# Perceiver block: cross-attention with smaller TensorE tiles for the scores and the weighted sums

## The chip, the core and the metric

The kernel runs on one core of a Trainium2 chip. The metric is the device time of one execution in microseconds (us), as the median over several runs.

## What is computed

A block of three layers works on `x` of 16 batch elements x 64 queries x 512. Only the first layer is touched, a cross-attention of 16 heads of 32 dimensions to a context of 1601 rows of 256 per batch element:

```python
y_dca, y_main = y[:, -16:], y[:, :-16]                 # 16 and 1585 context rows
k, v = (y_main @ Wk + bk), (y_main @ Wv + bv)           # per head, k is layer-normed over its 32 dimensions
ctx = softmax(q @ k.T * 32 ** -0.5) @ v                 # q is layer-normed per head too
ctx = ctx + softmax(q @ k_dca.T * 32 ** -0.5) @ v_dca   # the 16 last rows, with weights of their own
return ctx @ Wo + bo
```

A self-attention with 4 key heads and a mixture of 8 experts (2 for each token) follow.

## The kernel before

All of it is float32. The projections of the context are made from three products of halves in a reduced form (`split_product`, line 107); scores, transposes and weighted sums are plain float32 matmuls, each of which the trace shows as two pairs of one weight load (PEld, LDWEIGHTS) and one MATMUL.

`cross_attention` works through the 16 batch elements, two in a step i. The context of one element is cut into chunks of 128 keys: 12 full ones and a *tail* with what is left of the main rows and the 16 `dca` rows. Such a chunk is a *unit* u; a step has 26 units, of which 24 are full chunks and two are tails. Both tails share one projection. The units are taken in 12 *groups* a step: five groups of two units and one of three (the third is the tail) for each element. The table `GROUP` at the top of the file holds them.

Each engine has its own order of work, written out by hand in its `steps`, and semaphores join them. In the PE stream one group is: key projection, value projection and transposes of the normalised keys (`keys`, `values`, `turn`) for later groups; then the weighted sums (`weighted`, L1296) of this group's units, then the scores (`scores`, L1279) of the next group's units. ACT makes the exponentials of a group (`exps`, L1004) first of all in its turn, then copies values (L990), scales and stores the transposed keys (L976), rounds the context (L963) and gives the seeds of the reciprocal roots (L113, L115). DVE adds the key bias (L1133), reduces the squares (L1139) and normalises (L120 to L124, L1148). POOL squares (L1088) and makes the low halves of the context (L1081).

For a unit the scores are transposed: the stationary operand is the keys, the moving one the queries. `k32` holds 128 rows (4 heads x 32 dimensions), 4 groups of heads, 128 keys. `qbd` holds the queries in a block-diagonal form: rows of head r have their 64 queries in the column half r % 2 and zeros in the other half. A matmul takes 64 rows (two heads), 128 keys and 128 columns of `qbd`, and gives the scores of two heads: 8 matmuls a unit, alternating between the row tiles of rows 0 to 63 and 64 to 127. They fill two PSUM banks for 16 heads x 64 queries. The first unit of a group uses banks 3 and 4, the second 5 and 6, the tail 1 and 2, which are the value and transpose banks. An exponential of 128 x 1024 turns a unit's two banks into `probs`.

For the weighted sums the probabilities are stationary (128 keys x 64 queries of one head) and the values with a column of ones move (33 columns). Heads 2p and 2p + 1 go to the two column tiles of 64. That is 16 matmuls for a chunk and 32 for a tail, where the main rows and the `dca` rows are summed apart. Chunks accumulate in bank 7.

The kernel has a second form of its loops, taken when scores could grow large (`guarded`); the inputs here take the plain form, in which the PE program is written out for all steps.

A wait that the prediction speaks of, in the PE stream of groups 5 and 11 (the group after the scores of three units), before the first value projection into bank 1:

```python
if j == 0 and group in (5, 11):
    pe.wait_ge(s["ex"], unit(i, GROUP[group][-1]))
values(i, project[j])
```

Of the kernel before, what the change touches and what calls it, by code (L numbers as in the profile page):

```python
# [14 lines left out]
ACT = mybir.ActivationFunctionType  # L15
# [6 lines left out]
P = 128  # L22
B, SQ, D = 16, 64, 512
SK, DC, DCA = 1601, 256, 16
H, HD = 16, 32
# [10 lines left out]
GROUPS = H // 4  # L36
VW1 = HD + 1
VBUFS = 6
TAIL_ROWS, DCA_ROWS = (0, 64), (DCA_ROW, 0)
TAIL, PROJ, UNITS = LAST, 2 * CH - 1, 2 * CH  # L40
# [14 lines left out]
SCALE = HD ** -0.5  # L55
# [29 lines left out]
def transposes(pe, bank, src, ident, n=KD):  # L85

    for k in range(n):
        last = pe.transpose(bank[:, k * P:(k + 1) * P], src[:, k * P:(k + 1) * P], ident)  # L88
    return last
# [655 lines left out]

def cross_attention(nc, io, g, psum):
    K_BANK, V_BANK, TR_BANK, S_BANK, O_BANK = 0, 1, 2, 3, 7
    S_PLACES = (S_BANK, S_BANK + 2, V_BANK)

    with ExitStack() as ctx:  # L750
        def sb(name, shape, dt=F32):
            return ctx.enter_context(nc.sbuf_tensor(name, shape, dt))

        s = Sems(nc, ctx, "xa")
# [8 lines left out]
        k32 = g.k32  # L763
        probs = sb("probs", [P, 3, H * SQ])
        select = sb("select", [2, 3, P])
        shift_raw = sb("shift_raw", [2, H * SQ])
        shift = sb("shift", [2, H * SQ])
# [5 lines left out]
        def at(i, n, per):  # L773

            return (i, n) if n < per else (i + 1, n - per)

        def projected(i, n):

            i, n = at(i, n, PROJ)
            return i * PROJ + (PROJ + n + 1)  # L780

        def unit(i, u):

            i, u = at(i, u, UNITS)
            return i * UNITS + (UNITS + u + 1)

        def column(n):

            return n if n < CH else n - CH

        def proj_of(u):

            return TAIL if u == UNITS - 1 else u

        def tail(n):

            return column(n) == LAST

        def buf(n):

            return 2 if tail(n) else column(n) % 2

        def k_buf(u):

            return {TAIL: 2, UNITS - 1: 3}.get(u, column(u) % 2)
# [5 lines left out]
        def last_unit(u):  # L811

            return u - UNITS + CH if u == TAIL else u - CH if u == UNITS - 1 else u - 2 if column(u) >= 2 else u - 3
# [30 lines left out]
        blocks = [(slice(i * HD, (i + 1) * HD), slice(i % 2 * SQ, (i % 2 + 1) * SQ)) for i in range(4)]  # L844

        def parts(guarded):

            return 5 if guarded else 4

        def place(h):  # L850

            return (h // 2 % 2) * 8 + h // 4 * 2 + h % 2

        def projections(group, room):

# [19 lines left out]
        with nc.Block() as block:  # L875
# [69 lines left out]
            def _(act):  # L945
# [52 lines left out]
                               projected(i, n)).then_inc(s["kseed"], 1)  # L998

                def exps(i, u, j):  # L1000
                    act.wait_ge(s["sc"], unit(i, u))
                    act.wait_ge(s["pv"], unit(i, last_unit(u)))
                    bank = S_PLACES[j]
                    nc.scalar.activation(probs[:, buf(u), :], psum[:, bank:bank + 2, :].rearrange("p a n -> p (a n)"),  # L1004
                                         ACT.Exp, scale=SCALE).then_inc(s["ex"], 1)

                def o_evac(b, i, u):

# [216 lines left out]
            def _(pe):  # L1225
# [20 lines left out]
                def turn(i, n):  # L1246
# [2 lines left out]
                    pe.wait_ge(s["ke"], projected(i, n - 1))  # L1249
                    transposes(pe, psum[:, TR_BANK, :], kn[:, buf(n), :], g.ident[:]).then_inc(s["tr"], 1)  # L1250

                def scores(i, u, j, guarded, values_done=None, turned_done=None):
                    i, u = at(i, u, UNITS)
                    b = i * 2 + u // CH
                    pe.wait_ge(s["ke"], projected(i, proj_of(u)))
                    if j < 2:
                        pe.wait_ge(s["ex"], unit(i, u - 3 if column(u) < 2 else u - 2))
                    else:
                        pe.wait_ge(s["ve"], values_done)
                        pe.wait_ge(s["ke"], turned_done)  # L1260
                    if column(u) == 0:
                        pe.wait_ge(s["qb"], b * parts(guarded) + parts(guarded))
                        if guarded:
                            pe.wait_ge(s["select"], 16)
                    if tail(u):
                        pe.wait_ge(s["kd"], b + 1)
                    bank = S_PLACES[j]
                    out = [[psum[:, bank + a, n * P:(n + 1) * P] for a in range(2)] for n in range(GROUPS)]
                    if guarded:

                        for n in range(GROUPS):
                            for a in range(2):
                                pe.matmul(out[n][a], select[:, {TAIL: 1, UNITS - 1: 2}.get(u, 0), :],
                                          shift[:, (2 * n + a) * P:(2 * n + a + 1) * P],
                                          start=(n == 0), stop=False, skip_group_check=True)
                    for n in range(GROUPS):
                        for a in range(2):
                            rows = slice(a * 2 * HD, (a + 1) * 2 * HD)
                            last = pe.matmul(out[n][a], k32[rows, k_buf(u), n, :], g.qbd[rows, n, :],  # L1279
                                             start=not guarded, stop=True, skip_group_check=True)  # L1280
                    last.then_inc(s["sc"], 1)

                def weighted(i, u, latest):
                    half = u // CH
                    pe.wait_ge(s["ex"], unit(i, u))
                    pe.wait_ge(s["ve"], projected(i, latest if tail(u) else u))
                    if column(u) == 0:
                        pe.wait_ge(s["oe"], i * 2 + (half + 1))
                    if tail(u):
                        pe.wait_ge(s[f"vd{half}"], i * 16 + 16)  # L1290
                    for n in range(2 if tail(u) else 1):
                        for p in range(PAIRS):
                            for j in range(2):
                                h = 2 * p + j
                                v = g.v_last[:, half, n, h, :] if tail(u) else g.v[:, (u - half) % VBUFS, h, :]
                                last = pe.matmul(psum[j * SQ:(j + 1) * SQ, V_BANK if n else O_BANK, p * VW1:(p + 1) * VW1],  # L1296
                                                 probs[:, buf(u), place(h) * SQ:(place(h) + 1) * SQ], v,
                                                 start=(p == 0 and (column(u) == 0 or n == 1)), stop=tail(u), skip_group_check=True)
                    last.then_inc(s["pv"], 1)

                def turn_ctx(b):
# [26 lines left out]
                def steps(i, room, guarded):  # L1328
                    latest = PROJ - 1
                    for group in range(GR):  # L1330
# [28 lines left out]
                        for u in units(group, room):  # L1359
                            weighted(i, u, latest)  # L1360
                        for j, u in enumerate(units(group + 1, room)):
                            scores(i, u, j, guarded, projected(i, latest), projected(i, last_turned))
# [1184 lines left out]
```

## Time and profile before

| | |
|---|---|
| median of 3 runs | 1488.43 us (1487.6 to 1489.63) |
| profiled execution, span from first to last instruction | 1487.2 us |
| PE busy, matmuls | 1399.9 us (94%), 15754 matmuls |
| PE busy, weight loads | 1181.9 us (79%) |
| DVE, ACT, POOL busy | 860.5, 778.8, 500.8 us (58, 52, 34%) |
| mean granted TensorE clock | 0.977 of 2.4 GHz |

The profile gives no separate time for the profiled execution; its span is 1.2 us under the median of the runs. Times are microseconds unless marked ns. PE is the matmul side of TensorE, PEld its weight loads, which overlap; DVE is VectorE, ACT ScalarE, POOL GpSimd. A form such as 128*64 128x33 says: 128 rows and 64 columns of the array, moving operand of 128 partitions x 33 elements. The duration of a single matmul holds its way through the array too, so starts tell more than durations. A row of the timeline merges like instructions that follow each other, from the first start to the last end.

### The profile page before, as it was taken

What the parts mean: (1) busy time and instruction counts of PE and PEld (TensorE: products, weight loads), DVE (VectorE), ACT (ScalarE), POOL (GpSimd) and SP (SyncE); (2) the same over time, 40 slices, a digit from 0 to 9 for tenths busy, and PEclk for the clock granted to TensorE, in tenths of its full rate; (3) what the DMA queues carried; (4) which work ended last, traced back from release to release, by engine and by line L of the source; (5) the groups of instructions that cost most, each with busy time, mean ns of one, the idle gap of its engine ahead of it and who ended that gap; (6) DMA issues with size and microseconds to landing.
All of it is one profiled execution on the core that took longest, in us unless ns stands there. A gap on an engine that the chain in (4) does not pass through costs nothing. (4 is left out here: it accounts for less than half of the span.)

```text
span 1487.2 us, 41615 instructions
## 1 busy us (share of the span) xinstructions
PE 1399.9 (94%) x15754; PEld 1181.9 (79%) x15754; DVE 860.5 (58%) x2005; ACT 778.8 (52%) x1560; POOL 500.8 (34%) x550
## 2 busy tenths in 40 slices
PE   6789999999999999999999999999999899984796
PEld 3378888888888888888888888888878677764696
DVE  7756555655655565556456555655555356655764
ACT  2345555655555565555555555555555433333653
POOL 3333333333333333333333333333323121111455
PEclk9999999999999999999999999999999999995999
DMA  7042110210111121102101101211010100004886
GB/s 253 19 158 77 31 30 16 91 31 16 62 46 30 30 78 30 30 16 92 30 16 62 48 28 30 78 30 31 17 74 2 60 3 30 30 30 178 220 182 140
DMA packets 38937, 91.24 MB, mean 61 GB/s; under 512 B 8135, under 2 KB 11722, under 8 KB 37258
## 3 DMA queue, kind: packets, MB, share of 16 engines
q1 hardware_dynamic: 31904, 72.38, 14.5%
q0 software_dynamic: 6432, 16.32, 4.8%
q8 instruction: 133, 2.18, 0.6%
q14 instruction: 34, 0.28, 0.1%
q10 hardware_dynamic: 434, 0.08, 0.0%
HBM read 71.93 MB, written 36.01 MB: 73 GB/s over the span
## 5 line engine op out<-in xcount | busy, mean ns | idle before, releaser
L1088 POOL TENSOR_TENSOR ksq<-kc 128x512 f32<-128x512 f32 x200 | 208.4, 1042 | 423.8 <-DVE kc L1133 421.9
L1133 DVE TENSOR_TENSOR kc<-psum,bk_sb 128x512 f32<-128x512 f32 x200 | 138.3, 692 | 235.2 <-PE psum L107 234.7
L990 ACT COPY v_sb<-psum 128x512 f32<-128x512 f32 x192 | 112.7, 587 | 277.2 <-PE psum L107 277.2
L1004 ACT ACTIVATE probs<-psum 128x1024 f32<-128x1024 f32 x208 | 201.0, 1023 | 76.6 <-PE psum L1279 76.5
L1081 POOL TENSOR_TENSOR y_lo<-y_sb,y_hi 128x256 fp32r<-128x256 f32 x190 | 139.8, 736 | 231.4 <-ACT y_hi L963 231.3
L1279 PE MATMUL psum<-qbd,k 64*128 64x128 f32 x3328 | 211.9, 278 | 0.1
L1296 PEld LDWEIGHTS psum<-v_sb,probs 128*64 128x64 f32 x6144 | 187.4, 138 | 18.5 <-issue 18.5
L1139 DVE TENSOR_REDUCE kss<-ksq 128x16 f32<-128x512 f32 x200 | 136.5, 682 | 111.4 <-POOL ksq L1088 111.4
L1296 PE MATMUL psum<-v_sb,probs 128*64 128x33 f32 x6144 | 198.1, 224 | 0.0
L1279 PEld LDWEIGHTS psum<-qbd,k 64*128 64x128 f32 x3328 | 193.3, 188 | 4.5 <-ACT k L976 0.3
L107 PE MATMUL psum<-wk_hi,y_hi 128*128 128x512 f32 x400 | 176.8, 442 | 10.7 <-issue 8.6
L107 PE MATMUL psum<-wv_hi,y_hi 128*128 128x512 f32 x400 | 158.1, 395 | 2.9 <-ACT v_sb L990 2.2
L107 PE MATMUL psum<-wk_hi,y_lo 128*128 128x512 f32 x400 | 158.0, 395 | 0.0
L107 PE MATMUL psum<-wk_lo,y_hi 128*128 128x512 f32 x400 | 157.1, 393 | 0.0
L107 PE MATMUL psum<-wv_hi,y_lo 128*128 128x512 f32 x400 | 156.9, 392 | 0.0
L107 PE MATMUL psum<-wv_lo,y_hi 128*128 128x512 f32 x400 | 156.4, 391 | 0.0
L976 ACT ACTIVATE k<-psum,cols_sb 128x512 f32<-128x512 f32 x192 | 150.6, 784 | 10.6 <-PE psum L88 10.6
L1148 DVE SCALAR_TENSOR_TENSOR kn<-kc,kr 128x512 f32<-128x512 f32 x200 | 141.5, 707 | 7.0
L88 PEld LDWEIGHTS psum<-ident_sb,kn 128*128 128x128 f32 x800 | 98.9, 139 | 26.6 <-issue 0.5
L88 PE MATMUL psum<-ident_sb,kn 128*128 128x128 f32 x800 | 119.8, 272 | 0.0
L122 DVE SCALAR_TENSOR_TENSOR ktmp<-ktmp,kseed 128x16 f32<-128x16 f32 x200 | 115.6, 578 | 6.8
L107 PEld LDWEIGHTS psum<-wk_hi,y_hi 128*128 128x128 f32 x400 | 75.5, 189 | 29.3 <-issue 11.1
(272 smaller groups left out, 1983.9 us busy)
## 6 DMA issues: line engine op xcount, KB each, us to landing
y_sb<-in_y SPq DMA_DIRECT2D x48, 512.0 KB, 3.6
slots_dram<-in_blank SPq DMA_DIRECT2D x9, 2080.0 KB
expert_raw<-in_experts SPq DMA_DIRECT2D x8, 1024.0 KB, 6.9
x_sb<-slots_dram SPq DMA_DIRECT2D x23, 260.0 KB, 3.2
x_sb<-in_x SPq DMA_DIRECT2D x1, 1536.0 KB, 10.7
wq<-in_wq SPq DMA_DIRECT2D x4, 256.0 KB, 4.4
xa_wo<-in_wo SPq DMA_DIRECT2D x1, 1024.0 KB, 12.1
y_tail<-in_y_tail SPq DMA_DIRECT2D x8, 128.0 KB, 21.2
```

The costliest lines, as they stand in the source:

```text
L88: last = pe.transpose(bank[:, k * P:(k + 1) * P], src[:, k * P:(k + 1) * P], ident)
L107: last = pe.matmul(bank, lhs, rhs, start=(n == 0), stop=(n == len(todo) - 1))
L122: nc.vector.scalar_tensor_tensor(out=tmp, in0=tmp, scalar=-0.5, in1=seed, op0=ALU.mult, op1=ALU.mult).then_inc(second, 1)
L976: last = nc.scalar.activation(k32[:, buf(n)], bank, ACT.Identity, scale=g.cols[:, 2:3], bias=g.cols[:, 3:4])
L1004: nc.scalar.activation(probs[:, buf(u), :], psum[:, bank:bank + 2, :].rearrange("p a n -> p (a n)"), ACT.Exp, scale=SCALE).then_inc(s["ex" ...
L1081: nc.gpsimd.tensor_tensor(g.y_lo[:, buf(n)], src, g.y_hi[:, buf(n)].bitcast(F32), ALU.subtract).then_inc(s["ylo"], 1)
L1088: nc.gpsimd.tensor_tensor(sq[:, buf(n)], kc[:, buf(n)], kc[:, buf(n)], ALU.mult).then_inc(s["ksq"], 1)
L1133: nc.vector.tensor_tensor(kc[:, buf(n)], psum[:, K_BANK, :], g.bk[:], ALU.add).then_inc(s["kb"], 1)
L1139: nc.vector.tensor_reduce(ss[:, buf(n)], head_view(sq[:, buf(n)]), AX_X, ALU.add).then_inc(s["krd"], 1)
L1148: nc.vector.scalar_tensor_tensor(out=head_view(kn[:, buf(n)]), in0=head_view(kc[:, buf(n)]), scalar=HD ** 0.5, in1=spread(kr[:, buf(n)], H ...
L1279: last = pe.matmul(out[n][a], k32[rows, k_buf(u), n, :], g.qbd[rows, n, :], start=not guarded, stop=True, skip_group_check=True)
L1296: last = pe.matmul(psum[j * SQ:(j + 1) * SQ, V_BANK if n else O_BANK, p * VW1:(p + 1) * VW1], probs[:, buf(u), place(h) * SQ:(place(h) + 1 ...
```

## The change

The weighted sums take 32 queries as stationary columns instead of 64, so that four column tiles are used in turn, with twice the matmuls, for chunks and tails. The scores of full chunks take 32 rows (one head) and 64 keys as stationary and only the 64 columns of `qbd` that are not zero as moving operand: 32 matmuls a unit instead of 8, over four row tiles and two column tiles. The scores of row tile r go to a bank of their own, 3 + r, and the two units of a group share these four banks, by column halves. The order of heads in `probs` changes with it. As the banks are shared, the exponential of a group's first unit waits for the scores of its second, and the scores of a group's first unit wait for the exponential of the last chunk before. Tails keep the old form of scores, in banks 1 and 2.

```diff
-    S_PLACES = (S_BANK, S_BANK + 2, V_BANK)
+    TAIL_BANK = V_BANK
...
-        def place(h):
-
-            return (h // 2 % 2) * 8 + h // 4 * 2 + h % 2
+        def place(h, u):
+
+            return (h // 2 % 2) * 8 + h // 4 * 2 + h % 2 if tail(u) else h % 4 * GROUPS + h // 4
...
                 def exps(i, u, j):
-                    act.wait_ge(s["sc"], unit(i, u))
+                    act.wait_ge(s["sc"], unit(i, u + 1 if j == 0 else u))
                     act.wait_ge(s["pv"], unit(i, last_unit(u)))
-                    bank = S_PLACES[j]
-                    nc.scalar.activation(probs[:, buf(u), :], psum[:, bank:bank + 2, :].rearrange("p a n -> p (a n)"),
-                                         ACT.Exp, scale=SCALE).then_inc(s["ex"], 1)
+                    if tail(u):
+                        out, scored = probs[:, buf(u), :], psum[:, TAIL_BANK:TAIL_BANK + 2, :].rearrange("p a n -> p (a n)")
+                    else:
+                        out = probs[:, buf(u), :].rearrange("p (r n) -> p r n", r=4)
+                        scored = psum[:, S_BANK:S_BANK + 4, j * GROUPS * SQ:(j + 1) * GROUPS * SQ]
+                    nc.scalar.activation(out, scored, ACT.Exp, scale=SCALE).then_inc(s["ex"], 1)
...
+                def chunk_scores(u, j, guarded):
...
+                    at_n = [slice(j * GROUPS * SQ + n * SQ, j * GROUPS * SQ + (n + 1) * SQ) for n in range(GROUPS)]
...
+                    for n in range(GROUPS):
+                        for half in range(2):
+                            keys = slice(half * SQ, (half + 1) * SQ)
+                            for r in range(4):
+                                rows, cols = blocks[r]
+                                last = pe.matmul(psum[keys, S_BANK + r, at_n[n]], k32[rows, k_buf(u), n, keys],
+                                                 g.qbd[rows, n, cols], start=not guarded, stop=True, skip_group_check=True)
+                    return last
...
-                    if j < 2:
-                        pe.wait_ge(s["ex"], unit(i, u - 3 if column(u) < 2 else u - 2))
-                    else:
+                    if j == 0:
+                        pe.wait_ge(s["ex"], unit(i, u - 2 if column(u) == 0 else u - 1))
+                    if j == 2:
                         pe.wait_ge(s["ve"], values_done)
                         pe.wait_ge(s["ke"], turned_done)
...
+                    last = tail_scores(u, guarded) if tail(u) else chunk_scores(u, j, guarded)
                     last.then_inc(s["sc"], 1)
...
-                                last = pe.matmul(psum[j * SQ:(j + 1) * SQ, V_BANK if n else O_BANK, p * VW1:(p + 1) * VW1],
-                                                 probs[:, buf(u), place(h) * SQ:(place(h) + 1) * SQ], v,
-                                                 start=(p == 0 and (column(u) == 0 or n == 1)), stop=tail(u), skip_group_check=True)
+                                for part in range(0, SQ, HD):
+                                    last = pe.matmul(psum[j * SQ + part:j * SQ + part + HD, V_BANK if n else O_BANK, p * VW1:(p + 1) * VW1],
+                                                     probs[:, buf(u), place(h, u) * SQ + part:place(h, u) * SQ + part + HD], v,
+                                                     start=(p == 0 and (column(u) == 0 or n == 1)), stop=tail(u),
+                                                     skip_group_check=True)
```

`tail_scores` holds the lines of the old `scores` for the tail alone.

## Rows read from the trace of the kernel before

**Rows 1.** The page: span, busy time of each engine.

```profile
span 1487.2 us, 41615 instructions
PE 1399.9 (94%) x15754; PEld 1181.9 (79%) x15754; DVE 860.5 (58%) x2005; ACT 778.8 (52%) x1560; POOL 500.8 (34%) x550
```

**Rows 2.** Busy time by stretch: the cross-attention stage, then two successive groups.

```profile
core 0: us, PE busy (x) PEld busy (x) DVE busy (x) ACT busy (x) POOL busy (x), PEclk, DMA share, GB/s
75.00:1172.00 1097.00, 1091.05 (x13609) 942.89 (x13610) 615.56 (x1299) 627.88 (x1267) 382.97 (x443) 1.00 0.13 44
604.63:615.18 10.55, 10.55 (x130) 9.12 (x128) 5.86 (x12) 6.00 (x13) 3.55 (x4) 1.00 0.13 43
615.18:626.63 11.45, 11.45 (x146) 10.02 (x145) 5.87 (x12) 6.91 (x14) 3.56 (x4) 1.00 0.11 30
```

**Rows 3.** Groups by line and form: xcount, busy us, mean ns, idle before.

```profile
L1279 PE MATMUL psum<-qbd,k 64*128 64x128 f32 x3328 | 211.9, 278 | 0.1
L1296 PE MATMUL psum<-v_sb,probs 128*64 128x33 f32 x6144 | 198.1, 224 | 0.0
...
L1004 ACT ACTIVATE probs<-psum 128x1024 f32<-128x1024 f32 x208 | 201.0, 1023 | 76.6 <-PE psum L1279 76.5
...
L1296 PE MATMUL psum<-v_last,probs 128*64 128x33 f32 x1024 | 32.6, 223 | 0.0
...
L1966 PE MATMUL psum<-sa_xT,sa_wq 128*128 128x128 f32 x256 | 30.4, 278 | 0.0
...
L1991 PE MATMUL psum<-sa_kT,sa_qT 64*64 64x128 f32 x256 | 8.8, 275 | 0.0
...
L1310 PE MATMUL psum<-xa_wo,ctxT 128*128 128x512 f32 x16 | 7.3, 599 | 0.0
```

**Rows 4.** Timeline of a two-unit group: start us, us, instruction.

```profile
604.63 0.50 PE L107 MATMUL psum<-wk_hi,y_hi 128*128 128x512 f32 x1
...
611.21 2.06 PE L1296 MATMUL psum<-v_sb,probs 128*64 128x33 f32 x64
611.36 0.78 ACT L976 ACTIVATE k<-psum,cols_sb 128x512 f32<-128x512 f32 x1
...
613.20 2.06 PE L1279 MATMUL psum<-qbd,k 64*128 64x128 f32 x32
...
614.13 0.69 DVE L1148 SCALAR_TENSOR_TENSOR kn<-kc,kr 128x512 f32<-128x512 f32 x1
...
615.18 0.50 PE L107 MATMUL psum<-wk_hi,y_hi 128*128 128x512 f32 x1
...
616.97 0.69 DVE L1133 TENSOR_TENSOR kc<-psum,bk_sb 128x512 f32<-128x512 f32 x1 [2.14 <-PE psum L107]
```

**Rows 5.** Timeline of PE: other tile shapes.

```profile
1163.05 3.60 PE L1310 MATMUL psum<-xa_wo,ctxT 128*128 128x512 f32 x8
...
1192.86 3.74 PE L1966 MATMUL psum<-sa_xT,sa_wq 128*128 128x128 f32 x32
...
1198.31 1.10 PE L1991 MATMUL psum<-sa_kT,sa_qT 64*64 64x128 f32 x32
```

**Rows 6.** Busy time in slices, L1991 alone (self-attention scores, four tiles).

```profile
core 0: us, PE busy (x) PEld busy (x), PEclk, DMA share, GB/s
1198.31:1198.32 0.01, 0.01 (x2) 0.01 (x2) 1.00 0.00 0
1198.32:1198.33 0.01, 0.01 (x3) 0.01 (x3) 1.00 0.00 0
1198.33:1198.34 0.01, 0.01 (x4) 0.01 (x4) 1.00 0.00 0
1198.34:1198.46 0.12, 0.12 (x4) 0.12 (x8) 1.00 0.00 0
```

**Rows 7.** Timeline around the scores of three units.

```profile
623.75 2.95 PE L1279 MATMUL psum<-qbd,k 64*128 64x128 f32 x48
...
624.96 2.86 ACT L1004 ACTIVATE probs<-psum 128x1024 f32<-128x1024 f32 x3 [0.83 <-PE psum L1279]
626.63 0.50 PE L107 MATMUL psum<-wk_hi,y_hi 128*128 128x512 f32 x1
...
628.12 0.39 PE L107 MATMUL psum<-wv_hi,y_hi 128*128 128x512 f32 x1
```

**Rows 8.** Busy time in slices, L2020 alone (self-attention weighted sums).

```profile
1205.75:1205.78 0.03, 0.00 (x0) 0.02 (x1) 1.00 0.00 0
1205.78:1205.80 0.02, 0.01 (x2) 0.02 (x2) 1.00 0.00 0
```

**Rows 9.** DMA queue that carries PE's instructions: packets, MB, share of 16 engines.

```profile
q8 instruction: 133, 2.18, 0.6%
```

More of the change, by code:

```diff
@@ L1250, in turn, with tail_scores @@
                     transposes(pe, psum[:, TR_BANK, :], kn[:, buf(n), :], g.ident[:]).then_inc(s["tr"], 1)
+                def chunk_scores(u, j, guarded):
+                    at_n = [slice(j * GROUPS * SQ + n * SQ, j * GROUPS * SQ + (n + 1) * SQ) for n in range(GROUPS)]
+                    if guarded:
+                        for r in range(4):
+                            pe.matmul(psum[:, S_BANK + r, at_n[0].start:at_n[-1].stop], select[:, 0, :],
+                                      shift[:].rearrange("s (n r q) -> s n r q", n=GROUPS, r=4)[:, :, r, :],
+                                      start=True, stop=False, skip_group_check=True)
+                    for n in range(GROUPS):
+                        for half in range(2):
+                            keys = slice(half * SQ, (half + 1) * SQ)
+                            for r in range(4):
+                                rows, cols = blocks[r]
+                                last = pe.matmul(psum[keys, S_BANK + r, at_n[n]], k32[rows, k_buf(u), n, keys],
+                                                 g.qbd[rows, n, cols], start=not guarded, stop=True, skip_group_check=True)
+                    return last
+                def tail_scores(u, guarded):
+                    out = [[psum[:, TAIL_BANK + a, n * P:(n + 1) * P] for a in range(2)] for n in range(GROUPS)]
+                    if guarded:
+                        for n in range(GROUPS):
+                            for a in range(2):
+                                pe.matmul(out[n][a], select[:, {TAIL: 1, UNITS - 1: 2}[u], :],
+                                          shift[:, (2 * n + a) * P:(2 * n + a + 1) * P],
+                                          start=(n == 0), stop=False, skip_group_check=True)
+                    for n in range(GROUPS):
+                        for a in range(2):
+                            rows = slice(a * 2 * HD, (a + 1) * 2 * HD)
+                            last = pe.matmul(out[n][a], k32[rows, k_buf(u), n, :], g.qbd[rows, n, :],
+                                             start=not guarded, stop=True, skip_group_check=True)
+                    return last
                 def scores(i, u, j, guarded, values_done=None, turned_done=None):
@@ L1266, in scores @@
                         pe.wait_ge(s["kd"], b + 1)
[L1267 to L1280, printed above, removed]
+                    last = tail_scores(u, guarded) if tail(u) else chunk_scores(u, j, guarded)
                     last.then_inc(s["sc"], 1)
```

## Prediction

> **What bounds the kernel now.** I read the page's busy shares first [rows 1]: TensorE is busy 94% of the span, no other engine over 58%. As a busy share of pipelined matmuls can hide gaps, I then read busy time by stretch [rows 2]. In the cross-attention stage (75 to 1172 us) PE is busy 1091 of 1097 us at a granted clock of 1.00 (the 2.4 GHz level); ACT has 628 us of work, DVE 616, POOL 383. So any time that leaves the PE stream leaves the span, until another engine or a wait is late. The edits touch two groups of instructions there, which cost 198.1 + 32.6 us (weighted sums) and 211.9 us (scores) [rows 3]; projections and transposes stay.
>
> **How a tile pays.** Busy sums are too coarse to price a tile shape, so I read starts. A row of the timeline with N matmuls lasts (N - 1) spacings plus one mean duration. In [rows 4] the weighted sums, 64 matmuls on two column tiles, start every (2.06 - 0.223)/63 = 29.2 ns, 58.3 ns for a round of both tiles. The scores start every 0.89/16 = 55.6 ns by the difference of the x48 and x32 rows [rows 4, 7], 111.3 ns for a round on two row tiles. In [rows 5], with the mean durations of [rows 3], an untiled 128-column load with 128 moving columns takes (3.74 - 0.278)/31 = 111.7 ns; with 512 moving columns (3.60 - 0.599)/7 = 428.7 ns. The self-attention scores (64x64 tiles, four of them) take (1.10 - 0.275)/31 = 26.6 ns each, 106 ns per round of four.
>
> Two prices follow. Moving: (428.7 - 111.7)/384 = 0.83 ns per column plus 5.4 ns, so 33 columns cost 32.8 ns and 64 cost 58.2. Loading: 111.5 ns for 128 stationary columns and 58.3 for 64 (in the weighted sums, where moving costs only 33) give 0.83 ns per column plus 5 ns, so 32 columns cost 31.7. A round lasts as long as the larger of the two in one tile; other tiles run beside it. Third, the start of the next tile: slices of 10 ns from 1198.31 us on hold two, three and four matmuls, with as many loads (a count includes what still runs), and the following 0.12 us adds only four further loads [rows 6]: some 7 ns per pair, or 27 ns per round of four and 54 per round of eight, if this pace can be held.
>
> **Part by part.**
> 1. Weighted sums of chunks. 6144 pairs of load and matmul on two tiles are 3072 rounds of 58.3 ns = 179.1 us. After: 12288 pairs on four tiles, again 3072 rounds, of max(31.7, 32.8, 27) = 33 ns = 101.4 us. Saved: 77.7 us.
> 2. Weighted sums of tails. 1024 pairs, 512 rounds, become 2048 pairs, 512 rounds: 512 x 25.3 ns = 13.0 us saved.
> 3. Scores of chunks. 192 units of 16 pairs are 1536 rounds of 111.3 = 171.0 us. After: 12288 pairs on eight tiles (four row tiles, two column halves), 1536 rounds of max(58.3, 58.2, 54) = 58.3 ns = 89.5 us. Saved: 81.4 us. Tail scores (16 units) keep their form: nothing.
> 4. The later first exponential. It now waits for both units of the group. Before, it started 1.21 us after the first score (623.75 to 624.96), with one unit's 8 rounds of 111 ns done [rows 7]; now two units take 16 x 0.058 = 0.93 us, as one did, so it starts at about the same 1.2 us. Nothing needs the result before the next group's weighted sums, 6.6 us into a group (604.63 to 611.21) [rows 4]. Cost: nothing; with that cover gone, up to 0.93 us a group. ACT's queue behind it (value copies, from 3 us into the group) waits for projections anyway.
> 5. One wait loses its cover. In the groups with three units the first value projection of the next group reuses the tail's bank and waits for the third exponential. Before: exponentials end at 624.96 + 2.86 = 627.82, the values start at 628.12, 4.37 after the first score [rows 7]: 0.3 us of slack. After: scores end 0.86 us sooner, the values are ready to start at about 3.5 us, the exponentials end at 4.1 (2.86 us of work from 1.2 us on) plus about 0.1. New wait some 0.65 us, in 16 groups: 10.4 us given back. Queued behind it on PE: that projection, then the turns; DVE and POOL feed from them but have slack, below.
> 6. Exponentials read four banks of 256 columns instead of two of 512: same 1024 elements, 1024 ns [rows 3], no price seen for the stride; 5% more would be 10 us of ACT, hidden.
> 7. The new score waits (for the last exponential of the group before) are met some 5 us early. No DMA is moved; SP's and POOL's queues stay.
>
> Does the rest keep up? A two-unit group lasts 10.55 us [rows 2]; minus 2 x 16 x 25.3 ns and 2 x 8 x 53 ns = 1.66 it is 8.9. ACT has 6.0 to 6.9 us of work in one, DVE 5.9. The key chain: normalised keys end at 614.82, 10.19 us after the group's start at 604.63, and DVE's next job, the bias of the following group, starts at 616.97, 1.79 us after that group's start at 615.18 [rows 4]. After: 8.9 + 1.79 = 10.7, still after 10.19. Covered by 0.5 us; k (ACT, 611.36 + 0.78 = 612.14, 7.5 us in) is ready before the scores at 6.58 + 1.05 + 0.15 = 7.8.
>
> Sum: 77.7 + 13.0 + 81.4 - 10.4 = 161.7 us. The profiled span is 1487.2 us, 1.2 below the median of 1488.4; that goes on top. **1487.2 - 161.7 + 1.2 = 1326.7 us**, 10.9% less.
>
> **Against the skill.** The starts of [rows 6], which go to four different tiles, lie some 7 ns apart, while their average over the row is 26.6. The Trainium skill ("TensorE: Matmul & The Clock Gate", section "Wait — 56ns, not 53.3ns?") says that start to start never drops below about 25 ns however few columns move; by that rule a unit's 128 pairs would last 3.2 us, and the sum would be about 1774 us. The starts disagree with it; the average does not (the rival below has the row's figure in its place). The same page's section "Measured speedup vs the span model" prices a further tile at about 4 ns, and by that the sum stands; no run here shows sixteen tiles.
>
> **The rivals.**
> - *Instructions can't come that fast (slower).* Chunk weights and scores take 16 x 33 + 8 x 58.3 = 994 ns for 256 instructions, 3.9 ns each. The densest held flow that I found is 64 instructions in 0.83 us, 13.0 ns each [rows 5]; everything faster is a burst of eight. For: no row shows more, and the queue ahead of the array may hide the supply. Against: that flow is set by the tiles, as 106 ns is the price of 128 moving columns; and right after PE had stood idle, a matmul, a load and another matmul start within 1205.78 to 1205.80, faster than 13 ns each, if only three of them [rows 8]. If 13.0 ns were the limit, a unit's 256 instructions take 3.33 us instead of 16 x 58.3 + 8 x 111.3 = 1.82: +1.51 x 192, and 16 tails +1.46 each: +313 us, 1801 us. It decides from 1.82/256 = 7.1 ns per instruction: above, slower than before.
> - *Only part of the concurrency (faster by less).* (a) Eight tiles run as two fours: 27 ns more in 1536 rounds, +41, 1368. (b) Four loads of 128 rows overlap only by twos, the most seen at 128 rows [rows 3]: the round is 63 ns instead of 33, +30 x 3584 = +108, 1434; both (a) and (b), 1475. (c) Instructions arrive in pieces: 133 packets carry 2.18 MB, 16 KB each, and take 0.6% of 16 x 1487 us, 1.07 us apiece [rows 9]. Over PE's 31508 loads and matmuls [rows 1] that is at most 69 B each, so the new 512 small instructions of a group are about two packets, used in 2.0 us. If only one is held ahead, some 1 us is lost in 96 groups: 1423. Against: a group's average is one packet per 4 us.
> - *No change:* the shape is priced by the number of pairs only so far that gain and loss cancel; needs 7.1 ns exactly.
>
> **Bounds.** Low: rounds shrink to the start pace, 27 and 54 ns (-22 and -7), and the new wait is hidden (-10): 1288. High of the main case: rounds 10% longer (+21): 1348. High of the partial case: 1475.
>
> **Chances.** Main case 0.55 (1288 to 1348), partial 0.25 (1348 to 1475), no change 0.02, slower 0.18 (1491 to 1801). The range is the first two together, 1288 to 1478, and leaves out the last two, 0.20. A measurement here tells 0.2% (3 us) from nothing: faster 0.80, same 0.02, slower 0.18.
>
> **What would show it.** The weighted row of 128 matmuls for two units: 1.05 + 0.22 = 1.3 us; the scores row of 128: 0.93 us, the first round's start-up and 0.27, about 1.3 us. Two-unit groups of 8.9 us. A PE wait for ACT's exponential of about 0.65 us, 16 times. Rounds of eight as two fours 85 ns apart would mean (a). Starts evenly 25 ns or more apart would mean the supply, and the prediction is wrong from step 1 on.

## Result and the profile after

The changed kernel takes **1745.37 us** (median of 4 runs, 1738.66 to 1757.59) against 1489.03 for the kernel before on the same chip: ratio 1.173, 95% interval 1.168 to 1.178. It is 17% slower; the forecast was 11% faster, in a range that ended at 1478.

The head of the page, the queue that carries PE's instructions, and the slices of PE and its clock answer to [rows 1, 9]:

```profile
span 1736.8 us, 74203 instructions
## 1 busy us (share of the span) xinstructions
PE 1432.6 (82%) x32138; PEld 1170.2 (67%) x32138; DVE 861.6 (50%) x2005; ACT 781.0 (45%) x1560; POOL 500.6 (29%) x550
...
PE   7788888787888888888888888788888879994797
...
PEclk9899888988899888889888989999989889997899
...
q8 instruction: 260, 4.26, 1.0%
```

PE does twice as many matmuls and is now idle in the stage where it had hardly any gaps. The chain of waits of PE, longest sums first (waited for: us in total, times, longest):

```profile
PE psum L1269 <- issue: 170.7, 90, 2.7
PE psum L1321 <- issue: 41.7, 46, 2.8
...
PE psum L107 <- ACT probs L1008: 1.1, 4, 0.3
```

L1269 are the scores of chunks, L1321 the weighted sums. "issue" says that no semaphore, engine or DMA that the profile knows held PE; before, inside this stage, there was one such wait, of 0.7 us. By line and form (columns as in [rows 3]), projections (L107) included:

```profile
L107 PE MATMUL psum<-wk_hi,y_hi 128*128 128x512 f32 x400 | 202.8, 507 | 14.3 <-issue 12.1 <-DVE kc L1136 2.1
L1269 PE MATMUL psum<-qbd,k 32*64 32x64 f32 x12288 | 189.2, 245 | 171.3 <-issue 170.7 <-ACT k L976 0.4
L107 PE MATMUL psum<-wk_lo,y_hi 128*128 128x512 f32 x400 | 181.5, 454 | 1.2 <-issue 1.2
...
L1321 PE MATMUL psum<-v_sb,probs 128*32 128x33 f32 x12288 | 140.0, 198 | 14.9 <-issue 14.4
...
L1321 PE MATMUL psum<-v_last,probs 128*32 128x33 f32 x2048 | 24.9, 203 | 27.3 <-issue 27.3
```

The timeline of PE through two groups shows where the waits lie (most projections are left out; [rows 4] has a group of before):

```profile
700.63 0.71 PE L1269 MATMUL psum<-qbd,k 32*64 32x64 f32 x25 [2.18 <-issue]
...
702.18 0.63 PE L107 MATMUL psum<-wk_lo,y_hi 128*128 128x512 f32 x1
702.61 0.63 PE L107 MATMUL psum<-wk_hi,y_lo 128*128 128x512 f32 x1
...
710.44 1.37 PE L1321 MATMUL psum<-v_sb,probs 128*32 128x33 f32 x128
711.73 0.91 PE L1269 MATMUL psum<-qbd,k 32*64 32x64 f32 x64
714.48 0.90 PE L1269 MATMUL psum<-qbd,k 32*64 32x64 f32 x64 [1.84 <-issue]
715.32 0.50 PE L107 MATMUL psum<-wk_hi,y_hi 128*128 128x512 f32 x1
...
721.90 1.37 PE L1321 MATMUL psum<-v_sb,probs 128*32 128x33 f32 x128
723.20 0.47 PE L1269 MATMUL psum<-qbd,k 32*64 32x64 f32 x28
725.44 1.31 PE L1269 MATMUL psum<-qbd,k 32*64 32x64 f32 x100 [1.77 <-issue]
```

A scores burst stops in its middle, at no fixed head and with all operands ready, and goes on about 2 us later. The weighted row of 128 lasts 1.37 us; 1.3 was forecast. So the weighted sums are about as fast as forecast (the scores are slower, as priced further down), and something else is not. Three reads name it. First the stretches from one stall's end to the next:

```profile
core 0: us, PE busy (x) PEld busy (x) DVE busy (x) ACT busy (x) POOL busy (x), PEclk, DMA share, GB/s
700.63:714.48 13.85, 12.01 (x251) 9.83 (x251) 5.87 (x12) 6.30 (x13) 3.55 (x4) 0.79 0.02 6
714.48:725.44 10.96, 9.19 (x252) 7.66 (x251) 5.79 (x12) 6.04 (x12) 3.55 (x4) 1.00 0.04 7
725.44:740.82 15.38, 12.42 (x379) 10.37 (x380) 5.95 (x13) 6.04 (x12) 3.56 (x4) 0.88 0.12 37
```

They hold 502, 503 and 759 matmuls and loads: two, two and three times 251 to 253, though the times differ (the third has a group of three units). With the semaphore instructions of PE, which the trace records too, the count is 512, 512 and 768, and 134 of the 135 pauses inside bursts of small matmuls (starts more than 0.4 us apart; 239 us in sum, 1.77 each) come at one place of the count modulo 256, give or take one instruction. A packet of q8 is 4.26 MB / 260 = 16.4 KB. PE's instructions come in blocks of 256, and it stands at a block's end. Second, the packets themselves: the DMA view shows one of q8 in 711.9 to 712.1, none in 712.1 to 715.5, one in 715.5 to 715.7, none until 723.0, one in 723.0 to 723.3:

```profile
q8 instruction: 1, 0.02, 36.0%
```

The first starts at 711.96, 0.91 us after PE entered a new block (711.05, in the weighted sums), and PE can use it 2.53 us after its start, at 714.48. Over all pauses the resumption comes 2.44 us after a packet's start (5th to 95th percentile 2.20 to 2.75), and in the stage no two packets are less than 3.30 us apart. So a block is mostly fetched while the one before it is used. By the figures of this stall a fetch is over 0.91 + 2.53 = 3.4 us after PE entered the block before; that is an estimate of the least time that a block of 256 must last (13 ns per instruction) if PE is not to stand. Third, what follows a stall:

```profile
701.60:706.40 4.80, 4.80 (x13) 3.79 (x12) 0.69 (x2) 2.01 (x3) 1.04 (x1) 0.50 0.02 4
706.50:711.70 5.20, 5.20 (x150) 4.38 (x148) 3.44 (x7) 3.58 (x8) 1.78 (x2) 1.00 0.00 0
```

After the stall that ended at 700.63 the projections run at a granted clock of 0.50, the 1.2 GHz level, one per 0.43 us (702.18 to 702.61) instead of 0.23, for about 5 us. Not every stall is followed by this: the stretch from 714.48 on has 1.00. In all, the clock stands at 0.50 for 287 us between 75 us and the last scores; before it did so for 3 us.

**The 249.6 us of difference between the spans** (1736.8 - 1487.2) come out of the matmuls' starts in the two traces, each start to the next, summed by kind: scores with tails 205.3 before, 380.0 after, 191.2 of these in pauses; chunk sums 189.8 before, 148.0 after (20.5 pauses); tail sums 36.4, now 58.0 (29.4 pauses); projections 578.1, now 667.5; transposes and the rest +5.6. That is +174.7 - 41.8 + 21.6 + 89.4 + 5.6 = 249.5 us. The pauses take 241 (here those from 0.35 us on), the slow projections 89; nearly all of the 89 is clock, for 454 of the 2544 projections start at the 0.50 level, 12 before. Outside the pauses the scores save only 16.5 us, and behind pauses the tail's scores run slowly too (379 ns each by their row, before 278).

### The profile page after: what moved, and what is told of

Its sections match the earlier page's. It is cut to its first block and busy times, and to the rows that moved or that the text cites. A ratio compares the mean times of both kernels' runs of the same rounds, so it can differ in the third digit from the quotient of the medians.

```text
span 1736.8 us, 74203 instructions
## 1 busy us (share of the span) xinstructions
PE 1432.6 (82%) x32138; PEld 1170.2 (67%) x32138; DVE 861.6 (50%) x2005; ACT 781.0 (45%) x1560; POOL 500.6 (29%) x550
## 3 DMA queue, kind: packets, MB, share of 16 engines
q8 instruction: 260, 4.26, 1.0%
## 5 line engine op out<-in xcount | busy, mean ns | idle before, releaser
L1269 PE MATMUL psum<-qbd,k 32*64 32x64 f32 x12288 | 189.2, 245 | 171.3 <-issue 170.7
L1269 PEld LDWEIGHTS psum<-qbd,k 32*64 32x64 f32 x12288 | 161.4, 141 | 187.2 <-issue 182.6
L107 PE MATMUL psum<-wk_hi,y_hi 128*128 128x512 f32 x400 | 202.8, 507 | 14.3 <-issue 12.1
L107 PE MATMUL psum<-wk_lo,y_hi 128*128 128x512 f32 x400 | 181.5, 454 | 1.2 <-issue 1.2
L107 PE MATMUL psum<-wk_hi,y_lo 128*128 128x512 f32 x400 | 181.3, 453 | 0.9 <-issue 0.9
L107 PE MATMUL psum<-wv_hi,y_hi 128*128 128x512 f32 x400 | 170.9, 427 | 1.3 <-ACT probs L1008 1.1
L107 PE MATMUL psum<-wv_lo,y_hi 128*128 128x512 f32 x400 | 165.9, 415 | 0.0
L107 PE MATMUL psum<-wv_hi,y_lo 128*128 128x512 f32 x400 | 163.3, 408 | 0.0
L1321 PE MATMUL psum<-v_sb,probs 128*32 128x33 f32 x12288 | 140.0, 198 | 14.9 <-issue 14.4
L1321 PEld LDWEIGHTS psum<-v_sb,probs 128*32 128x32 f32 x12288 | 124.7, 109 | 36.8 <-issue 36.3
L107 PEld LDWEIGHTS psum<-wk_hi,y_hi 128*128 128x128 f32 x400 | 87.8, 220 | 37.3 <-issue 19.9
## 6 DMA issues: line engine op xcount, KB each, us to landing
y_tail<-in_y_tail SPq DMA_DIRECT2D x8, 128.0 KB, 21.4
```

The source lines that it names most:

```text
L107: last = pe.matmul(bank, lhs, rhs, start=(n == 0), stop=(n == len(todo) - 1))
L1269: last = pe.matmul(psum[keys, S_BANK + r, at_n[n]], k32[rows, k_buf(u), n, keys], g.qbd[rows, n, cols], start=not guarded, stop=True, skip ...
L1321: last = pe.matmul(psum[j * SQ + part:j * SQ + part + HD, V_BANK if n else O_BANK, p * VW1:(p + 1) * VW1], probs[:, buf(u), place(h, u) * ...
```

## The experiments

Theory A: blocks of 256 instructions, one fetched ahead. Theory B: the small tiles as such pause or cost. Theory C: every small instruction is served at an even 13 ns. The row of 1.37 us above already speaks against it: 128 weighted matmuls and their loads start within 1.17 us, 4.6 ns per instruction.

**One shape alone.** The weighted sums alone in the new form (the diff's last part, nothing else), then the scores alone (the rest of it):

> The weighted sums on four column tiles alone, scores as before. Theory A (PE's instructions come in blocks of 256, one block ahead, some 3.6 us from entering a block to having the next; a burst that uses a block faster stalls): a two-unit group has 384 small and large instructions; a stall of 1 to 2 us is met only when a block boundary falls in the first 70 or so of the weighted sums or just ahead of them, 0.35 us a group on the mean, 34 us in all, against 91 us saved: about 1432 us (1405 to 1470). Theory B (the eight-tile scores are slow by themselves, the weighted sums are as I priced them): 1489 - 91 = 1398 us, with no idle time that only 'issue' ends. Theory C (every small instruction is served at an even 13 ns): 256 x 13 ns = 3.3 us for the weighted sums of a group instead of 1.87, +1.5 us in 96 groups, 1630 us.

> The scores on eight tiles alone, weighted sums on two column tiles of 64 as before. Theory A: 384 instructions a group, 128 of them in the 1.9 us of the weighted sums ahead of the 256 of the scores; a boundary in either brings a stall of about 1.9 us in one group of three or more: 70 us lost, 81 saved, plus what a lower clock costs after stalls: 1480 to 1530 us. Theory B (eight-tile scores slow by themselves): all of the loss of the full change and none of the weighted sums' gain: about 1820 us. Theory C: 3.3 us instead of 1.8 in 96 groups: 1640 us.

Measured: weights alone 1496.53 us, ratio 1.004 [1.002, 1.006]; scores alone 1502.87, ratio 1.008 [1.006, 1.010]. Their waits on issue, the first two rows of the weights, the third of the scores:

```profile
PE psum L1297 <- issue: 43.0, 46, 2.8
...
PE psum L1279 <- issue: 13.1, 15, 2.0
```

```profile
PE psum L1269 <- issue: 27.5, 33, 1.6
```

Each part costs 7 or 13 us, both together 256. Nothing in either shape is dear by itself; with one shape new a group's burst has 256 dense instructions and the rest at the old pace, and the run has 61 or 34 pauses in bursts (69 and 35 us); with both new it has 512 at some 5 ns each, and 135 pauses (239 us). The weights alone missed every theory's number (1405 to 1470, 1398 and 1630 expected): A counted 34 us of pauses in groups of two units, and 69 came, 31 of them in the sums of tails, which it had left out. The scores alone lie in A's 1480 to 1530, but partly by luck: it counted 81 us saved and 70 lost, and both are about half that (37 and 35), with 13 us lost in projections.

**The same instructions in another order.** Both new shapes, the program of PE reordered so that units' sums and scores stand among the projections, in lots of 64 matmuls (355 of the 388 lots; the others, in groups with a tail above all, are larger):

```diff
+                                if j == 0:
+                                    for n, u in late:
+                                        scores(i, u, n, guarded)
+                                if j == 0 and group in (5, 11) or j == 1:
+                                    weigh()
                                 values(i, project[j])
+                                if j == 1 and to_score:
+                                    n, u = to_score.pop(0)
+                                    scores(i, u, n, guarded)
...
+                                if j == 0:
+                                    weigh()
```

> Both new shapes, with the same instructions, but PE's order changed: each unit's weighted sums and scores stand between the projections and transposes (key projection, the second unit's scores, value projection, transposes, weighted sums, key projection, weighted sums, value projection, scores, transposes), so that no more than 128 small instructions stand together in the two-unit groups; tail groups keep most of the old order. Theory A: 256 instructions then take 3.1 to 4.3 us of work, near the 3.6 us that a block needs, so most stalls vanish: 1330 to 1420 us. Theory B: the shapes cost what they cost, 1745 us. Theory C: 576 x 13 ns with nothing overlapped but the same sum as in the full change: about 1745 us too.

And the old shapes in this order, for the order's own price:

> The control for the order: the kernel before with only PE's order changed as in the spread version, old tile shapes and banks. All theories: 256 instructions a group were never short of supply, PE had no idle time, so within 10 us of 1489; a little more if a dependence (exponentials before weighted sums) is now late.

Measured: new shapes 1534.21 us, ratio 1.029 [1.025, 1.032]; old shapes 1614.06, ratio 1.083 [1.080, 1.085]. The issue waits of the new shapes:

```profile
PE psum L1321 <- issue: 11.3, 10, 2.1
```

With the same 32138 matmuls, in the same tiles, the time falls by 211 us and the pauses from 239 to 22 us. That refutes B (1745), though A's 1330 to 1420 is missed too. But the order itself costs 125 us, which I had put at nothing (expected 1489): each change between an untiled projection and tiled matmuls costs about 0.1 us, and PE waits 29 us for copies of keys. The old shapes have 582 more such changes in this order, some 58 us by that price; the rest of the 125 was not traced. At equal order the new shapes win 80 us, 5.0%.

**An order with fewer changes.** The chunk scores between the first key and value projection, the weighted sums between the second: bursts of 256 instructions with some 3 us of projections between them. In groups 1 and 7 the transposes of the context also stand behind the first key projection, and ACT copies it ahead of the exponentials; this holds for all three runs, and so is part of the order's price. With both new shapes, with the old ones, and with the new weighted sums alone:

```diff
                                 keys(i, project[j])
+                                if j == 0:
+                                    for n, u in late:
+                                        scores(i, u, n, guarded)
+                                if j == 1:
+                                    weigh()
+                                    weigh()
                                 values(i, project[j])
```

> Both new shapes, with the PE order of a group changed: key projection, the chunk scores of this group (put off from the group before), value projection, turn, second key projection, the weighted sums, second value projection, turn. So each burst of 256 small instructions stands between some 3 us of projections. Nothing is left out. Theory A (PE's instructions come in blocks of 256, one block ahead, a new one no sooner than 3.3 us after the last): a burst of 256 meets at most one block's end and the next block is mostly there, so stalls are under 40 us in sum instead of 239. Time 1363 us by the clean prices of the rows plus some 25 us of stalls and 20 us for one more change of tile form a group, 1395 to 1410 us, faster than before. Theory B (the stalls belong to the small tiles themselves, to their shapes or to loads beside matmuls): the same 239 us of stalls, 1745 us. Theory C (it is the changes between tile forms that cost): one more change a group than in the changed kernel, so slower than 1745 us.

> The kernel before with the PE order of the run above and the old shapes. Nothing is left out. This is the price of the order alone. Theory A: no issue waits; one more change of form in 96 groups and perhaps some waits for copies of keys, 1505 to 1525 us. If it were 1489 us, the order is free. If it is over 1560 us, the order has waits of its own, and the run above has to be read against this one.

> Only the weighted sums in four column tiles, scores in the old shape, with the order of the two runs above. Nothing is left out. Theory A: the scores' burst of 64 slow instructions no longer stands behind the weighted sums, so issue waits go from 56 to 43 us for the weighted sums and the last scores to under 15 us; 1405 to 1430 us. Theory B: the issue waits stay at 56 us and the order is paid on top, over 1510 us.

| order | old shapes | both new | weighted sums alone new |
|---|---|---|---|
| as before | 1489 | 1745 | 1497 |
| spread | 1614 | 1534 | - |
| split | 1530.63 [1.026, 1.030] | 1505.28 [1.009, 1.014] | 1479.88 [0.990, 0.996] |

(us, with the interval of the ratio to before.) The new shapes are 256 us slower, 80 faster or 25 faster than the old ones, by where the bursts stand. B's 1745 for both shapes is refuted again, and so is C of this expectation, more than 1745 by the changes of form. All three times are above what A expected, by 6, 95 and 50 us at least: the order costs 41 us where I had said up to 36, and the issue waits of both shapes together are 62, not 25:

```profile
PE psum L1269 <- issue: 39.6, 35, 2.2
PE psum L1321 <- issue: 22.2, 33, 2.3
```

Two blocks can still end within bursts a few us apart, and the fetch is not always prompt: over this stage a packet starts 1.1 us after a block is entered by the median, but 4.7 us after in one of 20 blocks. With the weighted sums alone this order is 0.7% faster than the kernel before.

**Only the worst bursts eased.** Weighted sums alone in the new form, old order, but in the 16 groups of three units the two chunks' sums go ahead of the second key projection (such a burst had 512 dense instructions and 64 old ones):

```diff
+                            if j == 1 and len(to_weigh) == 3:
+                                weighted(i, to_weigh.pop(0), latest)
+                                weighted(i, to_weigh.pop(0), latest)
                             if j < len(project):
```

> Only the weighted sums in four column tiles, old scores, old order, but in the groups of three units the weighted sums of the two full chunks go ahead of the second key projection, so that the burst at the group's end is 256 + 128 instructions as in the other groups, not 512 + 192. Nothing is left out. Theory A: the stalls in the sums of tails (31 us of the 69 in the run with the weighted sums alone) fall to about 10 us, for 16 more changes of form of some 0.3 us: 1497 - 21 - 0 + 5 = 1470 to 1485 us. Theory B: stalls stay, 1497 to 1503 us.

Measured 1483.69 us, ratio 0.995 [0.993, 0.998], inside A's range. Pauses in the tails' sums fell from 31.3 to 12.2 us. It too is a little faster than the kernel before, by 0.5%, with two calls moved.

**Fewer instructions in a burst.** The changed kernel with work left out. In the one, the second full unit of a group issues 8 of 64 pairs of sums and 8 of 64 of scores; in the other both units of every other group do. The other has `column(u) // 2 % 2 == 1` as its condition; `full` is set for the very first group. Both issue 21.4 thousand matmuls and have 176 packets:

```diff
+                def thin(u):
+
+                    return not tail(u) and column(u) % 2 == 1
...
-                    for n in range(GROUPS):
-                        for half in range(2):
+                    for n in range(GROUPS) if full or not thin(u) else (GROUPS - 1,):
+                        for half in range(2) if full or not thin(u) else (1,):
...
-                        for p in range(PAIRS):
+                        for p in range(PAIRS - 1 if thin(u) else 0, PAIRS):
```

> The changed kernel with work left out: of the second full unit of every group only 8 of 64 pairs of the weighted sums and 8 of 64 of the scores are issued. A group's burst is 288 small instructions instead of 512, in the same tiles and at the same density. Theory A (blocks of 256 instructions, one ahead, 3.3 us apart): hardly any burst needs two new blocks, stalls fall from 239 us to under 30 and the projections are back at the 2.4 GHz level; about 1370 us (the old time with the tile prices as measured) less 96 x 1.1 us left out = 1264, plus stalls: 1265 to 1300 us. Theory B (stalls belong to the small tiles, per instruction): 56% of them stay, 134 us and as much of the slow projections, 1410 to 1460 us.

> The same amount left out and the same count of instructions as in the run above, but from both full units of every other group: bursts of 512 and of 64 by turns. Theory A: each burst of 512 needs two blocks in 2.5 us with one ahead, so 48 groups stall some 2 us each, 80 to 130 us, and part of the projections behind them runs at 1.2 GHz: 1350 to 1420 us, 80 us or more above the run before. Theory B: the same time as the run before, within 10 us.

Measured: 1361.96 us (ratio 0.914 [0.911, 0.918]) and 1411.88 (0.947 [0.939, 0.955]). The rows are first those of the one, then of the other:

```profile
PE psum L1273 <- issue: 26.4, 30, 2.5
...
PE psum L1325 <- issue: 14.8, 13, 2.4
...
PE psum L107 <- ACT probs L1008: 6.3, 13, 1.1
```

```profile
PE psum L1273 <- issue: 52.9, 32, 2.3
...
PE psum L1325 <- issue: 13.0, 20, 2.5
```

The second run is not what its expectation says, bursts of 512 and of 64 instructions by turns. A burst holds the sums of one group and the scores of the next, so its bursts of two units have 128 sums + 16 scores and 16 + 128 by turns, and those of the first run 72 + 72: 288 instructions in either. The pair does not compare sizes of bursts.

The first run against the changed kernel does. In the 64 plain bursts of two units, 512 instructions have 78 pauses of 137 us in sum; 288 have 17, of 10 us. B's 56% would be 77 us, so it is refuted. A's sizes were off even so, and 1362 lies between its 1265 to 1300 and B's 1410 to 1460: the run has 54 us of pauses, not under 30, and its projections lose 33 us against before. 36 of the 54 us stand in the 15 bursts that hold a tail's sums, 256 dense instructions by themselves (the pause from 698.66 to 701.04 is one).

Between the two runs lie 50 us, 23 of it in pauses inside bursts (54 and 77), 16 in projections (611 and 628), at nearly equal counts of each shape and equal bursts. B's "within 10 us" is missed, and 1412 lies in A's 1350 to 1420 by luck, since the bursts of 512 that it was worked out from are not there. The 32 bursts of 16 + 128 have 23 us of pauses, more than all 64 of 72 + 72; why was not settled.

**More instructions without small parallel tiles.** The kernel before, with 128 tiny products a group, in one lot or in four:

```diff
+                def pad(n):
+                    for _ in range(n):
+                        pe.matmul(psum[0:8, O_BANK, 504:512], g.wk_hi[:, 0, 0:8], g.wk_hi[:, 0, 0:8],
+                                  start=False, stop=False, skip_group_check=True)
...
+                        pad(128)
                         for u in units(group, room):
```

> The kernel before, shapes and order as they are, with 128 tiny products added ahead of the weighted sums of every group (8 stationary and 8 moving columns, one place on the array, into 8 unused columns of bank 7; nobody reads them). About 256 more PE instructions a group, as many as the changed kernel has more. Nothing is left out. Theory A (blocks of 256 instructions, one ahead, 3.3 us apart): stalls appear though no tile got smaller and no second tile is used: 50 to 150 us of issue waits, mean 1 us or more, at one phase of the count modulo 256, some 260 packets of instructions; time 1489 us plus the products' own 100 to 200 us plus those waits. Theory B (the stalls belong to small tiles that run beside each other): no issue waits, 1489 us plus the products' own time.

> The same products in four lots of 32 behind the projections of the group instead of one lot of 128. Same count of instructions and packets (within 5%). Nothing is left out. Theory A: issue waits under 20 us. Theory B: none, as in the run before. The difference of the two runs is the price of density; some 0.1 to 0.2 us for each added change between projections and tiny products is paid here in either theory, up to 50 us.

Measured: 2116.01 us (ratio 1.420 [1.417, 1.424]) and 1847.37 (1.241 [1.238, 1.244]). Neither pauses on issue in a burst, with 229 and 231 packets. A's 50 to 150 us of such waits did not come. The runs don't tell A from B, though: on one tile such a product starts every 27 ns (3.46 us for 127 of them), 13.6 ns per instruction, 3.5 us for a block, and by the estimate of 3.4 us blocks come as fast as that. They do show that count alone is harmless at that pace. The dense form has another loss; its timeline and its stretches:

```profile
711.33 3.63 PE L1330 MATMUL psum<-wk_hi 128*8 128x8 f32 x128
714.89 3.63 PE L1296 MATMUL psum<-v_sb,probs 128*64 128x33 f32 x64
```

```profile
711.33:714.89 3.56, 3.56 (x131) 3.51 (x129) 2.76 (x8) 2.00 (x5) 1.10 (x2) 0.99 0.00 0
714.89:718.45 3.56, 3.56 (x68) 3.50 (x65) 0.32 (x1) 0.00 (x0) 0.00 (x0) 0.50 0.52 152
```

During the tiny products the granted clock is 0.99, right behind them 0.50, though PE was busy throughout, and the weighted sums take 3.63 us instead of 2.06 [rows 4]. So here the clock fell with no idle time ahead of it, behind 3.6 us of products of 8 stationary and 8 moving columns.

## Why the prediction was wrong

**The step that failed** is the term for the supply of PE's instructions, which the sum put at nothing. It cost 241 us in pauses, 2.5 us a group, and the slow clock behind many of them up to 89 more. Two rivals had it: that instructions can't come fast enough, put at 0.18, and (c), pieces of 16 KB with one held ahead, priced at 1 us a group. Both worked from the right rows. The mechanism is (c), which stood among the cases that are faster than before; its size is nearer to that of the first, so that 1745 lies between 1491 and 1801 is no merit of its reason. I set against it that "a group's average is one packet per 4 us": the average over 9 us of projections says nothing for 2.5 us in which two blocks are used up. The turnaround of 3.3 us stood in no row that I read: before, any 256 successive instructions of PE in this stage took at least 3.68 us, so no pause ever showed it. The 13.0 ns of [rows 5] as a limit was, by accident, nearly the rate at which blocks come; but a burst runs on what is held, so 512 instructions pay one or two pauses of 1.8 us, not 13 ns each. That is why 1801 was too high, and without the slow clock, which it did not have, it would be so by more.

**Term by term**, by clean stretches of the changed kernel and of the single-shape runs:

- Weighted round, forecast 33 ns: 128 matmuls start within 1.17 us, 9.2 ns per pair, 36.8 ns per round. Right within 12%, and rival (b), 63 ns, is out; the chunk sums without pauses fall by 62 us, not 77.7. Tails: 7.8 us without pauses, not 13.0.
- Scores round, forecast 58.3 ns: 128 start within 1.375 us, 10.8 ns per pair, 86.6 ns per round, 38 us saved of the 81.4. The first 32 or so start 6.7 ns apart but for one gap of 60 ns, as [rows 6] promised, and then the pace is 8.5 ns or worse. "If this pace can be held" was the doubtful clause. Rival (a)'s 85 ns is met in size, but the starts are not in two fours, so what sets that pace is open.
- Sum with these prices and no pauses: 1487.2 - 62 - 7.8 - 38 + 1.2, about 1381 us. Even without the supply I was 54 us too low.
- Wait for the tail's exponential, forecast 0.65 us in 16 groups: 1.1 us in all in the changed kernel, where PE is late anyway. With work left out and fewer pauses it is there, 6.3 us, 13 times, longest 1.1. Mechanism right, cover misjudged.
- The clock was in no step: [rows 2] showed 1.00 through the stage and I took it as given. It cost nearly all of the 89 us of projections. Behind 74 of the 101 pauses over 1 us it stood at 0.50 for at least 1.5 of the next 5 us, and the spread order, with the same matmuls and 22 us of pauses, has 14 us at 0.50 up to its last scores, not 287. So it goes with the pauses; but tiny products without idle time bring it down too, and how the 89 us divide between idle time and little work in the bursts was not separated.
- The later first exponential and the key chain cost nothing that a wait shows. Right.

The Trainium skill ("TensorE: Matmul & The Clock Gate", section "Wait — 56ns, not 53.3ns?") has start to start never below about 25 ns. The tiny products on one tile agree, 27 ns; on four and eight tiles 9.2 and 10.8 ns do not. By its 1774 us the rule came closest to 1745, by luck: in bursts between pauses the starts are 2.3 to 2.7 times denser than it allows.

**What stays open**: when exactly a packet is asked for (in the changed kernel mostly 0.9 to 1.9 us after a block is entered, at times much later), and what holds eight tiles at 10.8 ns per pair. It matters: of the blocks used up in under 2 us, 108 of 119 end in a gap of over 0.6 us in the changed kernel, but only 21 of 35 in the first run with work left out and 21 of 34 with the weighted sums alone. In the spared ones the next packet had started before the block was entered or at most 0.16 us behind, 0.8 us ahead by the median.

## What to carry to other kernels

Count instructions per burst, not per group or span: before cutting tiles smaller, divide the burst's time by its number of loads, matmuls and semaphore instructions; where 256 of them would pass in less than about 3.4 us (an estimate from fetches of this kernel; the blocks that paused were mostly used up in under 2), expect the next block to be late, and smaller tiles to be paid with pauses of 1 to 2.5 us, often with a slow clock behind them. Where such tiles do pay, place the bursts apart, between long matmuls, and price every added change of tile form. A stage at 100% busy and clock 1.00 shows the cost of neither, so test a denser burst before trusting the array's price.

## What the runs showed of the hardware

- PE's instructions arrive as 16 KB packets of 256; in this stage packets are at least 3.30 us apart (3.23 the least of any run), and PE goes on 2.44 us after the start of the one it stood for. A pause has no releaser in the trace ("issue") and recurs at one phase of the count.
- The granted clock fell to 0.50 not only behind idle time but behind 3.6 us of busy, tiny products.
- Reordering alone, with the same matmuls, cost 41 and 125 us. Part of it is that the first projections behind a tiled burst start 0.33 us apart instead of 0.23, and so do the last ones ahead of one.
